# Early-fusion transformer layer on one core: text tails issued ahead of the main text rows, class row laid in front of the text, first queries in two halves

## The reference, cut to what matters

```
def _L0_tok_ref(im, W, b, positions, cls_embedding):
    ...
    embeds = jnp.einsum('bsp,pd->bsd', patches, W) + b + pos
    cls_tok = jnp.broadcast_to(cls_embedding, (B, 1, EMBED))
    return jnp.concatenate((cls_tok, embeds), axis=1)
...
h = _L0_tok_ref(x, ...)
h = jnp.concatenate([h, txt], axis=1)
h = h + _L0_attn_ref(_layernorm(h, axis=-1), ...)     # 12 heads, Q = xn * W_qk, softmax(QQ'), @ W_o.T
h = h + _L0_ffn_ref(_layernorm(h, axis=-1), ...)      # 16 experts, top 4, and a shared one
return h
```

## Time and profile before

| | us |
|---|---|
| median of 3 runs | 445.6 |
| lowest, highest | 444.69, 446.07 |
| the profiled execution's own time | 445.42 |
| its span in the trace | 443.6 |

### The profile page before, as it was taken

The page is one execution under the profiler, slowest core; times in us unless marked ns, Lnnn a source line. Parts: engine busy times, 40 slices in busy tenths (PEclk is TensorE's granted clock), DMA queues, the critical chain, the costliest instruction groups (busy, mean ns, idle before and its releaser), DMA issues. The chain is left out here.

```text
span 443.6 us, 7087 instructions
## 1 busy us (share of the span) xinstructions
PE 424.7 (96%) x2425; PEld 358.1 (81%) x2425; DVE 317.9 (72%) x966; ACT 221.9 (50%) x642; POOL 105.6 (24%) x143
## 2 busy tenths in 40 slices
PE   8999999999999999999989999897989999999995
PEld 8787689877898667997669986786778888889994
DVE  5899865487655786447987869979776778656564
ACT  1766864447643466624653075763353643434432
POOL 4032112122212311210323347985410100000000
PEclk9999999999999999999999999999999999999999
DMA  5979999999999999996530053212042231323300
GB/s 183 300 265 199 213 213 213 213 214 212 214 212 214 213 213 213 214 213 175 215 132 2 0 192 88 69 45 64 6 127 92 74 80 27 98 84 90 82 26 36
DMA packets 20998, 63.61 MB, mean 143 GB/s; under 512 B 2572, under 2 KB 10964, under 8 KB 20578
## 3 DMA queue, kind: packets, MB, share of 16 engines
q0 software_dynamic: 7552, 39.39, 42.0%
q1 hardware_dynamic: 12546, 22.68, 16.9%
q10 hardware_dynamic: 864, 1.09, 0.8%
HBM read 61.88 MB, written 1.27 MB: 142 GB/s over the span
## 5 line engine op out<-in xcount | busy, mean ns | idle before, releaser
L645 ACT ACTIVATE area_p_r<-area_b 128x484 fp32r<-128x484 f32 (+1 forms) x51 | 30.7, 602 | 87.6 <-DVE area_b L1283 87.5
L574 ACT ACTIVATE area_p<-area_p,nmax 128x128 f32<-128x128 f32 x96 | 37.4, 390 | 73.3 <-DVE nmax L1172 73.3
L901 PE MATMUL bank<-area_t,area_o 128*128 128x192 f32 (+1 forms) x432 | 72.3, 327 | 0.0
L901 PEld LDWEIGHTS bank<-area_t,area_o 128*128 128x128 f32 (+1 forms) x432 | 69.8, 182 | 0.6 <-issue 0.6
L466 POOL DMA_DIRECT2D area_w<-in_L_attn_wte_dram x26 | 31.1, 1196 | 129.7 <-DMA area_w<-in_L_attn_wte_dram 129.7
L1269 DVE SCALAR_TENSOR_TENSOR area_b<-area_b,area_w 128x484 f32<-128x484 f32 (+1 forms) x36 | 27.4, 761 | 22.0 <-ACT area_b L668 19.9
L847 PE MATMUL bank<-area_p,xn 128*128 128x356 f32 x96 | 39.7, 495 | 0.0
L597 ACT ACTIVATE area_b<-xb,w 64x192 f32<-64x192 f32 x96 | 38.1, 444 | 0.8
L1170 DVE CUSTOM_DVE_ANT_0 area_p<-bank,cmask 128x128 f32<-128x128 f32 x96 | 23.9, 287 | 12.6 <-PE bank L800 12.6
L789 PE MATMUL bank<-area_a,xa 128*128 128x256 f32 x96 | 29.1, 385 | 0.5 <-DVE area_a L1160 0.4
L516 POOL TENSOR_TENSOR area_b_r<-area_b,area_p_r 128x484 fp32r<-128x484 f32 x17 | 21.9, 1290 | 31.2 <-ACT area_p_r L645 31.2
(11 more groups left out here) (266 smaller groups left out, 1072.0 us busy)
## 6 DMA issues: line engine op xcount, KB each, us to landing
area_w<-in_L_attn_wte_dram POOLq DMA_DIRECT2D x28, 1344.0 KB, 12.6
area_w<-gate_rows SPq DMA_DIRECT2D x24, 242.0 KB, 3.1
area_k<-in_experts_dram SPq DMA_DIRECT2D x8, 353.0 KB, 5.8
area_w<-gate_rows SPq DMA_DIRECT2D x12, 228.0 KB, 3.2
area_a<-in_experts_dram SPq DMA_DIRECT2D x6, 353.0 KB, 5.7
area_b<-gate_rows SPq DMA_DIRECT2D x8, 242.0 KB, 3.2
area_t<-in_L_attn_W_o_dram SPq DMA_DIRECT2D x1, 1728.0 KB, 11.4
area_o<-in_x_dram SPq DMA_DIRECT2D x4, 384.0 KB, 5.8
```

What stands on the lines that cost most here:

```text
L574: act.activation(pm[:, sl, n, :], pm[:, sl, n, :], ACT.Exp, scale=-1.0, bias=nmax[:, sl, n:n + 1], accum_out=psums[:, sl, n:n + 1])
L645: act.activation(hid_high[:, sl, 0:w], hidT[:, sl, 0:w], ACT.Copy).then_inc(hid_high_ready, 1)
L901: last = pe.matmul(o, oT[:, c, at:at + n], woT[:, c, :], start=(c == 0), stop=(c == NCH - 1))
```

## The change

The class row is laid in front of the text on the host, so `txt` has 129 rows. The main text rows and the class row come in one transfer to partitions 49 to 127, 79 of them. The tails (50 partitions) are issued ahead of the main rows, both after `s_zero`, and add to a semaphore of their own, `s_tails`. The class transfer is gone. DVE begins the variance of the tails on `s_tails[0]`, scales `lnw` ahead of `first_embed(0)`, and waits for `s_text[0]` only ahead of `variance((0,), ...)`. The first four heads' `qa` is formed by two instructions of two heads; PE starts the first two heads' scores on `qa_first`.

```diff
             def text_in(n, b0, b1):
-                sp.dma_start(hin[NIMG:P, b0:b1, 0, :], txt[0:TM, b0:b1, :]).then_inc(s_text[n], 16)
                 sp.wait_ge(s_zero, n + 1)
-                sp.dma_start(hin[0:TAIL, b0:b1, 1, :], txt[TM:NTXT, b0:b1, :]).then_inc(s_text[n], 16)
+                sp.dma_start(hin[0:TAIL, b0:b1, 1, :], txt[TM + 1:NTXT + 1, b0:b1, :]).then_inc(s_tails[n], 16)
+                sp.dma_start(hin[NPOS:P, b0:b1, 0, :], txt[0:TM + 1, b0:b1, :]).then_inc(s_text[n], 16)
 
             sp.dma_start(ximg[:, 0], x[0]).then_inc(s_x[0], 16)
             text_in(0, 0, 2)
-            sp.dma_start(hin[NIMG - 1:NIMG, :, 0, :], tok_cls[0].rearrange("a (c e) -> a c e", c=1)
-                         .broadcast_to([1, B, E])).then_inc(s_text[0], 16)
...
                     if U:
                         pe.wait_ge(max_of[k], U)
+                    elif k:
+                        queries_in(0, 0)
...
-            queries_in(0, 0)
+            pe.wait_ge(qa_first, 1)
             scores(0, 0)
...
-            dve.wait_ge(s_text[0], 48)
+            dve.wait_ge(s_tails[0], 16)
             variance((1, 3), OPENING[0])
             dve.wait_ge(s_pos, 32)
-            link(dve.tensor_tensor(postab[:], postab[:], tokb[:], ALU.add))
+            own.mark(dve.tensor_tensor(postab[:], postab[:], tokb[:], ALU.add))
+            dve.wait_ge(s_small, 32)
+            own.mark(dve.tensor_scalar(lnw[:], lnw[:], (1.0 + EPS) ** -0.5, None, ALU.mult))
+            dve.wait_ge(dve_own, own.at)
             dve.wait_ge(s_embps, 1)
-            link(first_embed(0))
+            own.mark(first_embed(0))
+            dve.wait_ge(s_text[0], 16)
+            dve.wait_ge(dve_own, own.at)
             variance((0,), OPENING[1])
-            dve.wait_ge(s_small, 32)
-            link(dve.tensor_scalar(lnw[:], lnw[:], (1.0 + EPS) ** -0.5, None, ALU.mult))
...
-            queries(0, 0, [0])
+            dve.wait_ge(xnT_ready, 1)
+            for j in range(0, GRP, 2):
+                keys = xa[:, 0, :].rearrange("p (c a t) -> p c a t", c=3, a=1).broadcast_to([P, 3, 2, 64])
+                scales = w2a[:, j:j + 2].rearrange("p (c j t) -> p c j t", c=1, t=1).broadcast_to([P, 3, 2, 64])
+                dve.tensor_tensor(qa[:, 0, :, j:j + 2, :], keys, scales, ALU.mult).then_inc(qa_ready if j else qa_first, 1)
...
-                        dve.wait_ge(s_text[1], 64)
+                        dve.wait_ge(s_text[1], 48)
+                        dve.wait_ge(s_tails[1], 16)
...
+    given['txt'] = _np.concatenate([_np.broadcast_to(given['L0_tok_cls_embedding'], (8, 1, 192)), given['txt']], axis=1)
```

More of the change, by code:

```diff
@@ L34, in mark, with early_fusion_kernel @@
         self.n += 1
-def early_fusion_kernel(nc, x, txt, tok_W, tok_b, tok_pos, tok_cls, ln_w, W_qk, W_o, wte,
+def early_fusion_kernel(nc, x, txt, tok_W, tok_b, tok_pos, ln_w, W_qk, W_o, wte,
                         gate_w, gate_b, bias, experts, bdown, rows, out):
@@ L41, in early_fusion_kernel @@
     NTXT, _, E = txt.shape
+    NTXT -= 1
     NPOS = 49
@@ L270, in early_fusion_kernel @@
         s_text = [sem("s_text_first"), sem("s_text_rest")]
+        s_tails = [sem("s_tails_first"), sem("s_tails_rest")]
         s_zero = sem("s_zero")
+        qa_first = sem("qa_first")
         s_embps = sem("s_embps")
@@ L368, in _ @@
             for k in range(2):
-                sp.dma_start(htail[TAIL * k:TAIL * k + TAIL, :, :], txt[TM:NTXT, k::2, :]).then_inc(s_text[1], 16)
+                sp.dma_start(htail[TAIL * k:TAIL * k + TAIL, :, :], txt[TM + 1:NTXT + 1, k::2, :]).then_inc(s_text[1], 16)
             sp.dma_start(woT[:], W_o).then_inc(s_wo, 16)
@@ L1569, in _ @@
             finish(NG - 1)
-_INS = ['x', 'txt', 'L0_tok_W', 'L0_tok_b', 'L0_tok_positions', 'L0_tok_cls_embedding', 'L0_attn_ln_w', 'L0_attn_W_qk',
+_INS = ['x', 'txt', 'L0_tok_W', 'L0_tok_b', 'L0_tok_positions', 'L0_attn_ln_w', 'L0_attn_W_qk',
         'L0_attn_W_o', 'L0_attn_wte', 'L0_ffn_gate_w', 'L0_ffn_gate_b', 'L0_ffn_bias', 'experts', 'bdown']
```

## The result

| | before | changed |
|---|---|---|
| median, us | 445.6 (5 runs beside it) | 463.68 (5 runs) |
| lowest, highest | 443.83, 446.57 | 462.63, 464.48 |
| profiled execution: time, span | 445.42, 443.6 | 463.68, 461.9 |

The ratio is 1.0402, 95% interval 1.0374 to 1.043. The change makes the kernel slower by 18.1 us; 463.4 was forecast.

The account below looks back on a forecast made before the run. The table stream, started by `W_o`'s landing, was taken to set the end from about 150 us on. 445.4 us plus 18.0 of stream delay gave 463.4, with PE's 12.9 covered and the head's gain about 0; range 456 to 471.

Parts of the forecast that it names:

- The single engine: Main text loads: 79 is prime, so each 79-partition transfer goes to a single DMA engine, shared with all other transfers.
- the reports up to the first pause: Sign in the changed kernel's trace: 4-byte reports in SP's queue up to its first pause would be 27, not 47.
- The price of a packet: On the one engine: 46 ns where the other engines are busy (to about 22 us), 36 ns elsewhere.
- The walk through the queue: Clogged engine's packets in SP's order: text seen at 13.9, x[2] at 35.6, `W_o` at 41.9, stream 18.0 us late.
- The stream carries it to the end, one to one: Table stream to the end: its 18.0 us delay covers PE's 12.9 and is passed on whole, giving 463.4 us.
- the first catch: Near 150 us: `rstd` for images 4 and 5 stands behind a table chunk, so DVE and PE wait for the stream.
- The head's gain: Start of PE's work: earlier `z` and first queries give 0.95 us, lost in longer waits for the stream, worth about 0.
- The queue that fills up: Rival, chance 0.08: SP can't issue x[2] to `W_o` until most of 474 packets are gone; 467 to 471 us.
- PE at half speed after a rest: PE's matmuls after idling might take twice the time, costing up to 2.4 us once more; taken as 0.

Follow-up runs that it names:

- 5 + 74: The changed kernel with the 79 main rows loaded by two transfers, of 5 and 74 partitions: 453.8 us, ratio 1.019.
- 15 + 64: The changed kernel with the 79 main rows loaded by two transfers, of 15 and 64 partitions: 446.48 us, ratio 1.0028.
- the first load whole: The changed kernel with only the text load of images 0 and 1 in one 79-partition transfer, the second split into 78 and 1 partitions: 448.27 us.
- the second load whole: The changed kernel with only the text load of images 2 to 7 in one 79-partition transfer, the first split into 78 and 1 partitions: 460.15 us.
- the nine rows of the table: Nine kernel versions whose table stream starts anywhere from 24 to 43 us; from there to the end each takes 418.7 to 419.7 us.
- `W_o` alone late: The changed kernel with text loads split into 78 and 1 partitions and SP waiting for image 0's third group of scores before issuing `W_o`: 454.86 us.
- the kernel before with 79: The kernel before with only the class row laid with the text and both main text loads as 79-partition transfers: 463.3 us, ratio 1.0396.
- 78 + 1: The changed kernel with the 79 main rows loaded by two transfers, 78 text rows and the class row: 445.98 us, ratio 1.0008.

## Why the prediction was right, point by point

The mechanism came out at every step that the time hangs on. That 463.4 and 463.68 lie within 0.3 us is in part luck: the stream started 0.87 us later than forecast, and from its start to the end it took 0.6 us less than before (419.1 against 419.7).

**The single engine: right.** The page's part on DMA queues has SP's as q1 (packets, MB, share of 16 engines). For the kernel before:

```profile
q1 hardware_dynamic: 12546, 22.68, 16.9%
```

For the changed kernel:

```profile
q1 hardware_dynamic: 12514, 22.68, 16.2%
```

For 5 + 74:

```profile
q1 hardware_dynamic: 12526, 22.68, 17.3%
```

Data packets are equal in number (78x8 and 8 before, 79x8 or (5+74)x8 now), so only reports can differ. Before, the loads in question had 13 + 13 + 8 = 34. With one engine for each 79-partition load there are 2, and 12546 - 32 = 12514. With 2 for 74 and 5 for 5, twice, there are 14, and 12546 - 20 = 12526. Both to the packet. The same count settles the other splits: 15 + 64 should have 62 reports and 12574 packets, the first load whole 20 and 12532, the second load whole 16 and 12528, and their profiles have just these numbers. I had named the reports up to the first pause as the test; that pause doesn't exist, since x[1] is issued at 9.03, before the first text has landed, and the whole run's count takes its place. On this the Trainium skill ("DMA: Bandwidth & Descriptors", section "Why a DMA increments its semaphore by 16 and not by 1") had the rule, the largest divisor up to 16, and the traces of 79 and of 74 agree with it.

**The price of a packet: right where the engine works alone, and put at the wrong times.** 36.4 ns is the spacing alone on the engine, where 36 was taken. But the forecast had it crowded (46 ns) to 22 us and quiet after that. In the run it was quiet from 14.5 to 28.4 and crowded after that, when SP's held-back transfers came: the last 100 packets or so took from 28.4 to 33.8, more than 50 ns each. The two errors cancel, so that the 474 packets end at 33.8 where 33.9 was forecast is luck in part.

By the figure for one engine in the Trainium skill ("DMA: Bandwidth & Descriptors", section "Specifications") the second load would have taken 12.6 us, an estimate. The row from 14.5 to 28 shows 371 packets of this queue in 13.5 us, so the measurement decides against it.

**The walk through the queue: right to a microsecond, with that help.** Text of images 0 and 1 seen at 13.40 (13.9 forecast), `z` at PE 15.89 (16.3), x[2] at PE 35.72 (35.6), PE 12.97 late there (12.9), `W_o` seen at 42.80 (41.9). The stream was 18.87 late, not 18.0: x[2] was on time to 0.1 us, so the error of 0.9 arose behind it, in x[3], `htail` or `W_o`'s eight long packets. No run measured these one by one.

**The stream carries it to the end, one to one: right, and the best supported step.** It rests on the nine rows of the table and on the run with `W_o` alone late. One detail was off: I put the first catch near 150 us. It comes one pair earlier, at 109.83 with 4.92 us. In POOL's timeline of before the `rstd` there is at 88.61, and DVE had no wait behind it:

```profile
88.61 1.51 POOL L459 TENSOR_TENSOR rs<-ve,mhalf 128x4 f32<-128x4 f32 x1
```

The stream's 19.7 us of delay outgrew PE's 14.3.

**The head's gain, 0.95 and swallowed: right on both, as far as the runs can tell.** With the load cured it is 0.83 us at `embed(1)` in the first profile and up to 1.65 in others with the same head, and the time stays within 0.3% of before. Without the stream's wait for `W_o` it is worth 1.26 us, by way of chunk 2. The five profiles with this head undisturbed have `embed(2)` at 21.09 to 21.92, the two with the old one at 22.75 and 22.83.

**The queue that fills up: a rival with 0.08 that came true in its mechanism and not in its price.** The forecast had SP issue `W_o` near 12 us; it was 30.25. But when SP was let go at 27.94, in the middle of its issues at L368, the clogged engine still had packets of the 474 to move until 33.8 (behind that no packet of 768 bytes shows until 36), so by the order of its queue `W_o` would be as late on it if issued at 12. That is worked out from the order; no run issued `W_o` early behind a clogged engine. The rival's extra up to 4 us, all engines starting `W_o` late, didn't show (and its 467 to 471 doesn't follow from it: 463.4 and up to 4 us more is at most 467.4): from 40 to 42 us only 3 packets started on all engines together. SP's queue in the changed kernel from 40 to 41 us:

```profile
q1 hardware_dynamic: 2, 0.03, 6.5%
```

And from 41 to 42 us:

```profile
q1 hardware_dynamic: 1, 0.01, 3.2%
```

The others had done their share beside the clogged one. So a forecast that treated "one engine is clogged" and "the queue is full" as separate cases was wrong to separate them: here they are one case with one price.

**PE at half speed after a rest: taken as 0, and wrong as a fact, right as a cost.** The changed kernel's busy times in stretches (us, PE busy, PEld, DVE, ACT, POOL busy, PE's granted clock, DMA share, GB/s):

```profile
15.00:18.00 3.00, 2.10 (x7) 1.45 (x8) 2.16 (x9) 0.72 (x3) 0.55 (x1) 0.50 0.07 21
18.00:21.00 3.00, 3.00 (x10) 2.82 (x9) 2.90 (x8) 2.92 (x9) 0.00 (x0) 0.50 0.07 21
21.00:24.00 3.00, 3.00 (x18) 2.02 (x18) 1.41 (x10) 0.59 (x3) 0.00 (x0) 0.92 0.08 24
...
32.00:36.00 4.00, 0.28 (x1) 0.28 (x2) 0.00 (x0) 0.02 (x1) 0.00 (x0) 0.50 0.98 319
```

After 4.71 us without a matmul PE came back at 1.2 GHz, and again after 7.39 us: `embed(2)` took 3.59 us, not 2.22. That is why PE waited 7.39 us for x[2] and not the 9 I had put: part of the hole was filled by slow matmuls. PE's delay grew from 12.97 to 14.34, still below the stream's 18.9, and so it cost nothing.

## What to carry to other kernels

Look at the number of partitions of a transfer before its bytes: by the rule that fits all counts here (78, 50, 79, 74, 64, 15, 5) a prime count above 16 puts it on one DMA engine, and everything issued behind it that uses all sixteen waits for that one. One row more in a transfer cost 18 us here, and one row less, sent by itself, gave them back. To price such a delay, don't follow the busy engine but the thing that already sets the end: here each microsecond by which the table stream started late was a microsecond at the end, and a faster head bought nothing until the stream's needless wait was gone and the head became what the stream waits for. Check that by the end of the chain, not by its start: it was the last chunk's time, not the stream's start, that gave the end in all twelve versions.

## What the runs showed of the hardware that I had not expected

- An issue on SP can block. Behind 474 packets for one engine the next issue took 17.74 us in the changed kernel and 16.91 in the kernel before with 79; two issues together took 16.62 with the second load whole and 7.37 behind 222 packets for each of two engines. Behind 158 for one the next took 4.75. In the changed kernel SP was let go at 27.94 with roughly 115 packets left on that engine: 474 and 30 of the tails, less 18 counted from 13.9 to 14.5 us and 371 to 28. No run here shows the depth by itself.
- A transfer of a single partition isn't bound to one engine: the 78 + 1 version has 12546 packets in SP's queue like the kernel before, which leaves 8 reports for its two one-partition loads of 2 and 6 rows, as with the 8 rows of the class transfer.
- TensorE was at its lower clock of 1.2 GHz after pauses of 4.71 and 7.39 us, and back at 0.92 of full speed on the mean from 21 to 24 us, after it had worked without a pause from 15.89 on.
